# Linear attention inside a graph network: where edge batches, bias adds and weight splits stand, and how squared norms are summed

## The reference, cut to what matters

```
for i in range(2):
    y = layernorm(x, ...)
    q, k, v = y @ Wq + bq, y @ Wk + bk, y @ Wv + bv
    qp = softmax_kernel(q, proj, True); kp = softmax_kernel(k, proj, False)
    o = (qp @ (kp^T v)) / (qp @ sum(kp))
    x = x + o @ Wo + bo
    x = x + gelu(layernorm(x) @ W1 + b1) @ W2 + b2
# softmax_kernel: exp(data_dash - diag - m) + eps,
#   diag = 0.5 * normalizer**2 * sum(data**2) per node and head, m = max of data_dash
```

## Time and profile before

| | us |
|---|---|
| median of 3 runs | 1929.31 (1927.92 to 1930.63) |
| the profiled execution's own time | 1926.08 |
| its span in the trace | 1924.2 |
| PE busy | 1749.6 (91%) |
| DVE busy | 1127.0 (59%) |
| POOL busy | 999.3 (52%) |
| ACT busy | 661.7 (34%) |

### The profile page before, as it was taken

The page is one execution under the profiler, slowest core; times in us unless marked ns, Lnnn a source line. Parts: engine busy times, 40 slices in busy tenths (PEclk is TensorE's granted clock), DMA queues, the critical chain, the costliest instruction groups (busy, mean ns, idle before and its releaser), DMA issues.

```text
span 1924.2 us, 21064 instructions
## 1 busy us (share of the span) xinstructions
PE 1749.6 (91%) x8251; PEld 1419.2 (74%) x8251; DVE 1127.0 (59%) x2029; ACT 661.7 (34%) x815; POOL 999.3 (52%) x540
## 2 busy tenths in 40 slices
PE   5989999999999799999999199999999959999996
PEld 4876778788788577888887177877778747887863
DVE  6585867999958467865346434233333276623275
ACT  3312333422331223343241255655556322120112
POOL 3213444356687667628771446676766481151402
PEclk9889979999988789999999599999999979999988
DMA  9252101256423212123243567777777341121101
GB/s 331 88 193 65 1 1 1 80 144 139 86 12 70 41 1 1 2 74 58 44 113 101 197 229 248 271 250 251 258 263 252 127 142 45 44 78 40 36 1 44
DMA packets 146786, 212.64 MB, mean 111 GB/s; under 512 B 43740, under 2 KB 60352, under 8 KB 145440
## 3 DMA queue, kind: packets, MB, share of 16 engines
q1 hardware_dynamic: 98736, 177.49, 27.9%
q0 software_dynamic: 42832, 18.84, 7.9%
q10 hardware_dynamic: 5120, 14.99, 2.2%
HBM read 187.21 MB, written 30.08 MB: 113 GB/s over the span
## 4 chain that ended last, share of the span: by engine, by line
PE 69%; DVE 17%; POOL 4%; issue 4%; DMA 3%; ACT 3%; SPq 0%; POOLq 0%; DVEq 0%
PE PS L634 18%; PE PS L636 18%; PE PS L635 18%; PE PS L795 4%; PE PS L783 3%; PE PS L766 3%; DVE G L1675 2%; DVE nqmax L1671 1%; POOL table_w L2272 1%; PE PS L677 1%; DMA table_c<-edge_add,edge_ix 1%; POOL table_c L2272 1%; DVE G L1543 1%; DVE h_op L1927 1%; POOL slots_x L2306 1%
## 5 line engine op out<-in xcount | busy, mean ns | idle before, releaser
L2199 POOL TENSOR_TENSOR W<-raw,W 128x2048 fp32r<-128x2048 f32 x40 | 192.1, 4806 | 332.5 <-ACT W L1163 332.5
L2272 POOL DMA_INDIRECT table_w<-edge_add,edge_ix x128 | 209.0, 1633 | 72.4 <-DMA table_w<-edge_add,edge_ix 41.6
L2272 POOL DMA_INDIRECT table_c<-edge_add,edge_ix x128 | 203.3, 1588 | 60.7 <-issue 34.4
L634 PE MATMUL PS<-op_b,W 128*128 128x512 f32 x576 | 226.9, 394 | 3.6 <-DVE op_b L2006 2.5
L635 PE MATMUL PS<-op_b,W 128*128 128x512 f32 x576 | 225.8, 392 | 0.0
L636 PE MATMUL PS<-op_b,W 128*128 128x512 f32 x576 | 225.6, 392 | 0.0
L634 PE MATMUL PS<-W,op_a 128*128 128x512 f32 x480 | 188.8, 393 | 1.8 <-DVE op_a L1736 1.8
L635 PE MATMUL PS<-W,op_a 128*128 128x512 f32 x480 | 187.8, 391 | 0.0
L636 PE MATMUL PS<-W,op_a 128*128 128x512 f32 x480 | 187.7, 391 | 0.0
L2311 POOL TENSOR_TENSOR W<-raw,W 128x2048 fp32r<-128x2048 f32 x30 | 143.4, 4791 | 56.4 <-ACT W L1372 56.4
L1163 ACT ACTIVATE W<-raw 128x2048 fp32r<-128x2048 f32 x40 | 76.5, 1921 | 156.3 <-PE PS L636 103.8
(11 more groups left out here) (417 smaller groups left out, 3956.0 us busy)
## 6 DMA issues: line engine op xcount, KB each, us to landing
raw<-in_L_ffn_w_dram SPq DMA_DIRECT2D x46, 1024.0 KB, 5.6
raw_e<-in_L_ffn_w_dram SPq DMA_DIRECT2D x22, 1024.0 KB, 5.5
raw_v<-in_L_ffn_w_dram SPq DMA_DIRECT2D x22, 1024.0 KB, 5.1
raw<-in_L_mix_W_dram SPq DMA_DIRECT2D x16, 1024.0 KB, 6.1
raw<-table_c SPq DMA_DIRECT2D x10, 1024.0 KB, 5.2
key_row<-key_dram SPq DMA_DIRECT2D x32, 256.0 KB, 3.9
w_row<-in_edge_weight_dram SPq DMA_DIRECT2D x32, 256.0 KB, 4.7
table_w<-zero POOLq DMA_DIRECT2D x4, 1024.0 KB, 7.9
```

Source lines behind the costliest of these rows:

```text
L634: pe.matmul(ps, lhs_hi, rhs_hi, start=start, stop=False)
L2199: pool.tensor_tensor(lo_at, raw[:, r % 2, :], hi_at.bitcast(F32), ALU.subtract).then_inc(lo_done, 1)
L2272: pool.indirect_dma_start(out=tb, out_offset=bass.IndirectOffsetOnAxis(ap=edge_ix[:, i, c:c + 1].bitcast(U32), axis=0), in_=edge_add[:, i, ...
```

## The change

The diff touches the q, k and v stages and the head pairs of both layers. In words:

- Norms: `head_sel` becomes 8 columns for each of 4 feature blocks and is now the stationary operand, and the squares move past it, 512 nodes at a time (`head_rows`). The result is 8 rows; ACT copies them to `d_rows`, and 8 small transposes (`head_columns`) bring them back. The rows of q stand after the first k job, the columns after the third; those of k after the first and second v job.
- Edge batches of layer 0: three in q, three in k. The bias bo is added inside the q stage, one tile after each square.
- `vsum`: DVE adds the v tiles into `v_sum`, and TensorE does one matmul.
- The splits of wo and of the first up move into the head pairs, on ACT and on POOL, and the scatter steps of layer 1 before the head pairs become 4, 6 and 11.

```diff
-EARLY_BATCHES = 6
+EARLY_AT = [(0, 1), (0, 3), (0, 6), (1, 2), (1, 4), (1, 6)]
# TensorE
+            def head_rows(x, l, i):
+                for c in range(2):
+                    n = JOB_AT[f"r{x}{l}", c]
+                    pe.wait_ge(squared, 16 * l + 8 * i + 4 * c + 4)
+                    open_job(n)
+                    for m in range(NK):
+                        mm = pe.matmul(bank(n)[0:HEADS, :], head_sel[:, m, :], G[:, 4 * c + m, :], start=(m == 0), stop=(m == NK - 1))
+                    mm.then_inc(job_full, 1)
+            def head_columns(x, l):
+                for t in range(NT):
+                    if t % 4 == 0:
+                        evacuated(f"r{x}{l}", t // 4 + 1)
+                    mm = pe.transpose(bank(n)[:, t * HEADS:(t + 1) * HEADS], d_rows[:, t * P:(t + 1) * P], ident[0:HEADS, 0:HEADS])
+                        if i == 1 and j == 0:
+                            head_rows("q", l, 0)
+                        if i == 1 and j == 2:
+                            head_columns("q", l)
+                    if t == 0:
+                        head_rows("k", l, 1)
+                    if t == 1:
+                        head_columns("k", l)
-                for t in range(NT):
-                    mm = pe.matmul(bank(n), eps_ones[:, :], G[:, t, :], start=(t == 0), stop=(t == NT - 1))
+                pe.matmul(bank(n), eps_ones[:, :], v_sum[:, :], start=True, stop=True).then_inc(job_full, 1)
# ACT
-                split_hi(f"wo{l}")
-                split_hi(f"up{l}.0")
                 for hp in range(HEADS // 2):
+                    if hp == 1:
+                        split_hi(f"wo{l}")
...
+                    if hp == 2:
+                        split_hi(f"up{l}.0")
# DVE, q and k
-                        if i == 1 and j == 0:
-                            dve.wait_ge(job_full, JOB[f"dq{l}"] + 1)
+                        if i == 1 and j % 4 == 0:
+                            dve.wait_ge(job_full, JOB_AT[f"rq{l}", j // 4] + 1)
                         dve.tensor_tensor(G[:, j, :], at, at, ALU.mult).then_inc(squared, 1)
+                        if l == 0 and (i, j) in EARLY_AT:
+                            edge_batch(EARLY_AT.index((i, j)))
+                        if i == 0:
+                            ins = dve.tensor_tensor(X[:, j, :], X[:, j, :], rowv[:, row_at[f"bo{l}"] % 3, :], ALU.add)
# DVE, v
+                        dve.tensor_copy(V[:, :, :, DH], dexp[:, 1, :, :])
+                    if t:
+                        ins = dve.tensor_tensor(v_sum[:, :], G[:, 0, :] if t == 1 else v_sum[:, :], G[:, t, :], ALU.add)
# POOL
-                for name in ("wq", "wk", "wv", "wo"):
+                for name in ("wq", "wk", "wv"):
-                        scatter({"wq": 4, "wk": 6, "wv": 8, "wo": 5}[name])
-                lo(f"up{l}.0")
+                        scatter({"wq": 4, "wk": 6, "wv": 11}[name])
                 for hp in range(HEADS // 2):
                     pool.partition_all_reduce(kmaxp[:, 1, :], kmaxp[:, 0, :], P, bass.bass_isa.ReduceOp.max).then_inc(kmax_all, 1)
                     scatter(9 if l else 6)
+                    if hp == 0:
+                        lo(f"wo{l}")
+                    if hp == 1:
+                        lo(f"up{l}.0")
```

More of the change, by code:

```diff
@@ L40 @@
 EG = 8
-EARLY_BATCHES = 6
+EARLY_AT = [(0, 1), (0, 3), (0, 6), (1, 2), (1, 4), (1, 6)]
+EARLY_BATCHES = len(EARLY_AT)
 MLP_BATCHES = 6
@@ L109, in job_plan @@
             stages.append((f"q{l}", 8, "A"))
-        stages += [(f"dq{l}", 1, "A"), (f"k{l}", 8, "A"), (f"dk{l}", 1, "A"), (f"v{l}", 8, "D"), (f"vsum{l}", 1, "A")]
+        stages += [(f"k{l}", 1, "A"), (f"rq{l}", 2, "A"), (f"k{l}", 2, "A"), (f"dq{l}", 1, "A"), (f"k{l}", 5, "A"),
+                   (f"v{l}", 1, "D"), (f"rk{l}", 2, "A"), (f"v{l}", 1, "D"), (f"dk{l}", 1, "A"), (f"v{l}", 6, "D"), (f"vsum{l}", 1, "A")]
         for hp in range(HEADS // 2):
@@ L318, in gps_network @@
         eps_ones = place("eps_ones", [P, P])
-        head_sel = place("head_sel", [P, 2])
+        head_sel = place("head_sel", [P, NK, HEADS])
+        d_rows = place("d_rows", [HEADS, N], F32, at_e)
+        v_sum = place("v_sum", [P, D], F32, at_e + 4096)
         proj_nat = place("proj_nat", [P, 2, 2, DH])
@@ L727, in projection_job @@
                 mm.then_inc(job_full, 1)
+            def head_rows(x, l, i):
[7 more added lines that the diff above has]
+            def head_columns(x, l):
+                n = JOB[f"d{x}{l}"]
+                open_job(n)
+                for t in range(NT):
+                    if t % 4 == 0:
+                        evacuated(f"r{x}{l}", t // 4 + 1)
+                    mm = pe.transpose(bank(n)[:, t * HEADS:(t + 1) * HEADS], d_rows[:, t * P:(t + 1) * P], ident[0:HEADS, 0:HEADS])
+                mm.then_inc(job_full, 1)
             projection_job(0)
@@ L1241, in _, with rows_out, columns_out @@
             split_hi("wk0")
+            def rows_out(x, l):
+                for c in range(2):
+                    n = JOB_AT[f"r{x}{l}", c]
+                    act.wait_ge(job_full, n + 1)
+                    act.activation(d_rows[:, c * HALF:(c + 1) * HALF], bank(n)[0:HEADS, :], ACT.Copy).then_inc(job_act, 1)
+            def columns_out(x, i, l):
+                n = JOB[f"d{x}{l}"]
+                act.wait_ge(job_full, n + 1)
+                act.activation(dexp[:, i, :, :].rearrange("p t h -> p (t h)"), bank(n)[:, 0:NT * HEADS], ACT.Exp,
+                                   scale=-1.0).then_inc(job_act, 1)
             for l in range(DEPTH):
@@ L1251, in _ @@
                                        bias=colv[:, l, 8 + 4 * i + m:9 + 4 * i + m]).then_inc(job_act, 1)
+                        if i == 1 and j == 0:
+                            rows_out("q", l)
+                        if i == 1 and j == 2:
+                            columns_out("q", 0, l)
                         if i == 0 and l and j == 2:
@@ L1255, in _ @@
                             split_hi(f"wv{l}")
[L1256 to L1259, removed]
-                split_hi(f"wo{l}")
-                split_hi(f"up{l}.0")
[L1262 to L1267, removed]
+                rows_out("k", l)
+                columns_out("k", 1, l)
                 n = JOB[f"vsum{l}"]
@@ L1272, in _ @@
                     s = f"{l}.{hp}"
+                    if hp == 1:
+                        split_hi(f"wo{l}")
+                        if l == 0:
+                            act.wait_ge(zeroed, 144)
+                            for at in range(0, CHUNKS * P, HALF):
+                                n = min(HALF, CHUNKS * P - at)
+                                act.dma_start(slots_x[at:at + n, :].rearrange("(a b) d -> a (b d)", a=P // 2),
+                                              slots_y[0:n, :].rearrange("(a b) d -> a (b d)", a=P // 2)).then_inc(slots_zeroed, 16)
+                    if hp == 2:
+                        split_hi(f"up{l}.0")
                     for t in range(NT):
@@ L1635, in _ @@
                         dve.wait_ge(job_act, ACTS[n])
-                        if i == 1 and j == 0:
-                            dve.wait_ge(job_full, JOB[f"dq{l}"] + 1)
+                        if i == 1 and j % 4 == 0:
+                            dve.wait_ge(job_full, JOB_AT[f"rq{l}", j // 4] + 1)
                         dve.tensor_tensor(G[:, j, :], at, at, ALU.mult).then_inc(squared, 1)
-                        if l == 0 and i == 1 and j not in (0, 2):
-                            edge_batch(0 if j == 1 else j - 2)
+                        if l == 0 and (i, j) in EARLY_AT:
+                            edge_batch(EARLY_AT.index((i, j)))
+                        if i == 0:
+                            if j == 0:
+                                row_wait(f"bo{l}")
+                            ins = dve.tensor_tensor(X[:, j, :], X[:, j, :], rowv[:, row_at[f"bo{l}"] % 3, :], ALU.add)
+                            if j == 7:
+                                link(ins)
                         if l == 1 and j % 2 and 8 * i + j > 5:
                             edge_batch(LATE_BATCH - 3 + 4 * i + j // 2)
[L1643 to L1646, removed]
                 row_wait(f"bv{l}")
@@ L1650, in _ @@
                 for t in range(NT):
-                    n = JOB[f"v{l}"] + t
+                    n = JOB_AT[f"v{l}", t]
                     dve.wait_ge(job_full, n + 1)
@@ L2207, in _ @@
             pool.memset(vsum[:, :, DH:VW], KERNEL_EPS * N)
-            link(pool.memset(head_sel[:, :], 0.0))
-            pool.memset(head_sel[0:DH, 0:1], 0.5 * NORMALIZER ** 2)
-            link(pool.memset(head_sel[DH:P, 1:2], 0.5 * NORMALIZER ** 2))
+            link(pool.memset(head_sel[:, :, :], 0.0))
+            for m in range(NK):
+                pool.memset(head_sel[0:DH, m, 2 * m:2 * m + 1], 0.5 * NORMALIZER ** 2)
+                ins = pool.memset(head_sel[DH:P, m, 2 * m + 1:2 * m + 2], 0.5 * NORMALIZER ** 2)
+            link(ins)
```

21 lines of the change are left out of this document (7 added, 14 removed).

## The result

| | before | after |
|---|---|---|
| median | 1929.97 (1927.92 to 1937.45, 4 runs) | 1963.22 (1960.66 to 1963.51, 4 runs) |
| the profiled execution's own span | 1924.2 | 1961.4 |
| PE busy | 1749.6 | 1755.9 |
| POOL busy | 999.3 | 996.9 |
| issue / POOL in the chain that ended last | 4% / 4% | 10% / 10% |

A forecast was written before the change was run, and what follows sets the result against it. TensorE holds most of the chain of waits, and POOL's round trips were to set the head pairs' pace. 4.0 + 13.9 + 3.4 = +21.3 on 1926.08, 1947.4; with 3.2 for the median 1950.6, said as 1950, range 1930 to 1962.

The forecast's parts named there:

- layer 0, pass 1: Second time DVE's nkmax passes POOL's all-reduce in layer 0: all-reduce 1 at 207.2, a wait of about 1 us.
- layer 1, distances: Time between successive nkmax passes in layer 1: two POOL cycles of 54.0 us, then 45.5 us.
- layer 1 in all: Layer 1's head pairs: last pass at 789.7 against 775.81, counted as +13.9 us.
- tail: Layer 1's MLP: two more scatter steps, 7.4 us, less 2.0 and 2.0 of slack, +3.4 us; bounds 0 and 5.
- Norms and squares in layer 0: Layer 0's q, k, v stages: at most -21.1 us, less waits of 2.4 and 9.3 and 2.6 lower clock, taken as -6.5.
- Round trips on POOL: Head pairs: two more trips per layer between all-reduce and low split, 7.9 us one way, up to 6.95 the other.
- Rival (a): POOL's gaps belong to a first use and don't come again; some 1896 us; chance 0.08.
- Rival (b): Clock stays up after waits, so pass 3 follows after 35 us; 1926 to 1930 us; chance 0.12.
- Layer 0's cycle: POOL from all-reduce to all-reduce in layer 0's head pairs: 22.9 + 6.95 + 4.6 + 7.9 = 42.4 us.
- Pass 3 of layer 0: Layer 0's last nkmax pass: 45.5 us after pass 2, at 295.5 against 291.52, +4.0 us.
- the 45.5: Interval in us from pass 2 to pass 3 in each layer, after waits for POOL; bounds 34.8 and 47.2.
- Layer 1's start: Layer 1's first nkmax pass, after 11 scatter steps and 7.9 us of gap: 636.2 against 656.14, -19.9 us.

The follow-up runs named there:

- switch_alone: Kernel before plus one small POOL subtraction (128 x 8) after the scatter steps of head pairs 0 and 1 in both layers, nothing moved; 1.0110, 1949.65 us.
- copies_back: Changed kernel with only ScalarE's six copies of slots_y into slots_x back ahead of layer 0's head pairs; 1.0118, 1950.18 us.
- late_lows: Changed kernel, copies back, both low splits after all-reduce 3, three more scatter steps in layer 0's MLP; 0.9883, 1907.54 us; again 0.9866, 1901.65.
- late_before: Kernel before with splits and scatter counts placed late, low splits after all-reduce 3; old norms, edges, bias adds, v sum; 0.9932, 1915.07 us.

## Why the prediction was right, and where its size failed

On the clock of the spans, after minus before. The prediction gave pass 1 of layer 0 only by its all-reduce (207.2, so some 207.6); it is set against the 212.71 above, the others against the earlier trace rows.

| step | predicted | measured |
|---|---|---|
| layer 0, pass 0 | -6.5 | -6.3 |
| layer 0, pass 1 | -5.1 | +13.8 |
| layer 0, pass 3 | +4.0 | +18.9 |
| layer 1, pass 0, beyond layer 0's shift | -19.9 | -26.6 |
| layer 1, distances | 54.0, 54.0, 45.5 | 53.7, 54.2, 47.5 |
| layer 1 in all | +13.9 | +9.1 |
| tail | +3.4 | +9.2 |
| sum | +21.3 | +37.2 |

*Norms and squares in layer 0: the waits right, the total in part by luck.* TensorE waits for VectorE's squares twice, where 2.4 and 9.3 were worked out:

```profile
84.14 5.92 PE L740 MATMUL PS<-G,head_sel 128*8 128x512 f32 x8 [4.38 <-DVE G L1677]
...
96.79 6.42 PE L740 MATMUL PS<-G,head_sel 128*8 128x512 f32 x8 [6.73 <-DVE G L1677]
...
574.04 7.03 PE L740 MATMUL PS<-G,head_sel 128*8 128x512 f32 x16
```

11.1 together against 11.7. The moving squares kept the clock where nothing waits: both halves together take 7.03 us (the last row, layer 1), 6.9 predicted. Behind the waits they did not: 5.92 and 6.42 us, where half of 7.03 is 3.5, at a granted clock of 0.63 from 84 to 97 us. That is 5.3 us lost, and the sum had 2.6, for one of the two gaps. The -6.3 came out all the same because TensorE ended k's first job at 79.76 and not at the 82.4 that was worked out: it began the q jobs 2.0 us earlier than in the kernel before (55.03 against 57.02). No term had that, and no run tells why.

*Round trips on POOL: right*, in both directions and in layer 1 to 0.3 us in the cycle. `switch_alone` shows the cause by itself. Rival (a), gaps of a first use only, is out: each of the six changes to the low split has its pair of MODIFY_POOL_CONFIG, and six go back. Rival (b) is out, and not by layer 1's 47.5 us alone. In all kernels of this case 12 passes waited 1.6 us or more for POOL and were followed by one that did not; the distance was 46.0 to 47.5 us each time, at a granted clock of 0.66 to 0.74. After passes without a wait it was 34.8 to 45.5.

*Layer 0's cycle: the term that failed.* "Six scatter steps end 22.9 us after an all-reduce starts" took the earlier trace rows as they were. They took 41.2 (164.91 to 206.14), because the copies moved in beside them. The diff shows the six transfers moving with the split of wo, and no term of the sum had them. `copies_back` puts them back: all-reduce 1 at 209.42 instead of 226.07 (207.2 predicted), and 12 us of the end. At the end of layer 0 the sum is 14.9 us short, out of 16 in all. The copies alone are 16.9: with them back pass 3 stands at 293.50, 2.0 earlier than the 295.5 of the sum.

*Pass 3 of layer 0.* 37.7 us followed pass 2, not 45.5; the 46.2 came one pass earlier, behind the 18.42 wait. In `copies_back` it is the same: 46.0 us behind the 1.59 us wait at pass 1, longer than POOL's cycle, so that nobody waited for POOL at pass 2, and then 37.7. The sum had the 45.5 one interval too late, and the error cancels in part.

*Layer 1's start.* 6.7 us better than predicted, from three parts on POOL. Its all-reduce 0 came after 5.85 us of library change instead of 7.9. Of layer 0's 18.9 us only 16.1 were left when its low split of wv began (573.13 before, 589.25 after). And the first eight scatter steps after it took 36.5 us instead of 39.8, of which the prediction had counted some 1 us.

*Tail.* POOL's `hg` low splits start 34.6 us later than in the earlier trace rows, 6.6 beyond the last pass's shift, and TensorE waits:

```profile
1035.90 0.77 PE L638 MATMUL PS<-op_b,W 128*128 128x512 f32 x1 [4.76 <-POOL W L2246]
1036.46 0.63 PE L639 MATMUL PS<-op_b,W 128*128 128x512 f32 x1
```

3.4 was the size of such a wait alone; it measured 4.76. The two rows also show products at 0.63 to 0.77 us after it instead of 0.39; by the gate transposes 7.9 us are lost. A wait of TensorE was priced at its length, and costs the slower clock behind it too. In the window from 1030 to 1063 us, the first row here, the granted clock is 0.90. The second row is the start of the graph product in the kernel before, at 1.00:

```profile
1030.00:1063.00 33.00, 28.24 (x115) 22.82 (x114) 15.95 (x17) 8.74 (x7) 18.21 (x4) 0.90 0.75 245
```

```profile
1002.00:1030.00 28.00, 28.00 (x125) 23.19 (x124) 11.16 (x21) 5.62 (x5) 12.59 (x3) 1.00 0.77 252
```

What stays open: the last 1.3 us between the gate and the end, the 2.0 us at the start, and how much of what the copies cost is their contention and how much the clock behind the wait that it made.

## What to carry to other kernels

On GpSimd count the changes between kinds of operation, not only the operations: 0.2 us of work at the wrong place cost 13 us of POOL each time. Put work that nobody waits for behind the last result that someone does: with both low splits there, and three scatter steps moved, `late_lows` took some 45 us less than `copies_back` by the two ratios, with one round trip a layer instead of three, and `late_before` 12.5 us less than the kernel before, with as many round trips. When a block of code moves, list every DMA that moves with it and what small transfers it will meet. A stretch in which an engine gets faster is also a stretch in which other things now coincide: look which SBUF operations of VectorE fall under GpSimd's. Not only those with two inputs suffer: in the kernel before a copy of 128 x 8 took 4.57 us (at 136.66) beside a low split, and 0.17 otherwise.

## What the runs showed of the hardware that I had not expected

- Small indirect transfers from POOL land after 3 us alone, and after 11 to 12 us beside 6 MB of DRAM to DRAM copies. The step that waits for them stood 17.3 us.
- The level of TensorE's clock in the head pairs isn't fixed by the kernel. `late_lows` twice, from its first to its second pass of layer 0 with no wait for POOL: 43.9 us in the first execution, 39.3 in the second, at a granted clock of 0.79 and 0.90 over the same window; these are the two rows, first execution first:

```profile
165.00:214.00 49.00, 47.39 (x213) 36.42 (x212) 33.46 (x77) 17.11 (x24) 21.95 (x16) 0.79 0.11 1
```

```profile
165.00:214.00 49.00, 46.39 (x245) 35.29 (x244) 37.99 (x85) 21.69 (x27) 27.18 (x19) 0.90 0.14 1
```

At the full clock the distance is 34.8: `late_lows` has it between its second and third pass (214.54 to 249.31), inside this row:

```profile
214.00:250.00 36.00, 34.31 (x204) 25.37 (x203) 29.43 (x71) 15.82 (x21) 19.88 (x15) 1.00 0.14 1
```

So the term for a head pair has a spread of its own of several us where no pass waited. Behind a wait for POOL it is narrow, 46.0 to 47.5, and the prediction's 45.5 lies just under it; what in the wait keeps the clock down for so long no run told.
